# Softmax reciprocals repeated through DRAM, and the value product of a pair ahead of the next score products

## The reference

```python
h = rmsnorm(x, norm_scale)
q, k, v = h @ wq, h @ wk, h @ wv            # 16 heads of 64
weights = softmax((q * 64 ** -0.5) @ k.T)   # per head, 256 x 256, float32
new_vals = weights @ v
x = layernorm(x + new_vals @ w_out + b_out)
```

## Time and profile before

| | us |
|---|---|
| median of 3 runs | 1432.15 (1431.54 to 1432.47) |
| the profiled execution | 1431.51 |
| its span | 1429.7 |

### The profile page before, as it was taken

How to read it: one execution, slowest core, us unless ns; L and a number is a source line. 1 busy time by engine, 2 the same in 40 slices (tenths; PEclk the granted TensorE clock), 3 DMA queues, 4 the chain that set the end, 5 groups by cost and what they waited for, 6 DMA issues and landing times.

```text
span 1429.7 us, 33458 instructions
## 1 busy us (share of the span) xinstructions
PE 1366.9 (96%) x11456; PEld 1202.2 (84%) x11456; DVE 925.6 (65%) x2535; ACT 904.3 (63%) x2492; POOL 502.5 (35%) x409
## 2 busy tenths in 40 slices
PE   6897999999999999999999999999999999999867
PEld 4685989888898988889898898988889898888767
DVE  4366576675766757566675757667576675756684
ACT  6675766757577575766657576675757657575423
POOL 3307062350705316071440706235070531607100
PEclk9999999999999999999999999999999999999988
DMA  7000000000000000000000000000000000000000
GB/s 262 5 1 5 1 2 8 0 7 0 0 7 0 7 0 0 7 0 7 0 7 0 0 7 0 7 0 7 0 0 7 0 7 0 0 5 1 5 1 8
DMA packets 13944, 13.77 MB, mean 10 GB/s; under 512 B 1609, under 2 KB 12754, under 8 KB 13650
## 3 DMA queue, kind: packets, MB, share of 16 engines
q1 hardware_dynamic: 13906, 13.27, 2.9%
HBM read 11.17 MB, written 2.10 MB: 9 GB/s over the span
## 4 chain that ended last, share of the span: by engine, by line
PE 64%; issue 11%; DVE 8%; ACT 4%; DVEq 4%; POOL 3%; POOLq 2%; SPq 1%; DMA 1%; ACTq 0%
PE bank_F L1208 14%; PE bank_S L1081 6%; DVEq L346 4%; PE bank_T L1067 4%; PE bank_T L1122 4%; PE bank_A L1135 4%; PE bank_T L1068 3%; PE bank_T L1069 3%; PE bank_F L1067 3%; ACT probs L573 3%; PE bank_F L1068 3%; PE bank_F L1069 3%; PE bank_A L1146 3%; PE bank_A L1067 3%; PE bank_A L1068 3%
## 5 line engine op out<-in xcount | busy, mean ns | idle before, releaser
L1208 PE MATMUL bank_F<-down,hid 128*128 128x128 f32 x2944 | 357.5, 277 | 5.4 <-DVE x L790 4.6
L1208 PEld LDWEIGHTS bank_F<-down,hid 128*128 128x128 f32 x2944 | 342.0, 192 | 14.7 <-DVE x L790 8.3
L573 ACT ACTIVATE probs<-bank_S,neg_max 128x256 f32<-128x256 f32 x512 | 236.2, 476 | 140.7 <-DVE neg_max L711 140.7
L711 DVE TENSOR_REDUCE neg_max<-bank_S 128x2 f32<-128x512 f32 x256 | 164.6, 684 | 96.1 <-PE bank_S L1081 96.0
L790 DVE SCALAR_TENSOR_TENSOR x<-bank_F,gates,x 128x128 f32<-128x128 f32 x496 | 149.8, 343 | 42.5 <-PE bank_F L1208 32.6
L491 POOL TENSOR_TENSOR hid<-hid,qkv 128x1024 f32<-128x1024 f32 x60 | 169.2, 2831 | 22.6 <-ACT hid L589 22.6
L461 POOL TENSOR_TENSOR mean_sq<-sum_sq,one_over_d 128x2 f32<-128x2 f32 x16 | 3.1, 197 | 442.8 <-ACT h_row L547 442.8
L552 ACT ACTIVATE probsT<-bank_T 128x512 f32<-128x512 f32 x256 | 139.6, 606 | 27.8 <-PE bank_T L1122 27.8
L479 POOL TENSOR_TENSOR hid<-qkv 128x1024 f32<-128x1024 f32 x45 | 121.1, 2690 | 69.3 <-ACT qkv L552 69.3
L1146 PE MATMUL bank_A<-probsT,values 128*64 128x256 f32 x1024 | 139.6, 394 | 1.1 <-ACT probsT L552 1.0
L1122 PE MATMUL bank_T<-ident,probs 128*128 128x128 f32 x1024 | 138.3, 278 | 0.2 <-ACT probs L573 0.2
(11 more groups left out here) (187 smaller groups left out, 3133.2 us busy)
## 6 DMA issues: line engine op xcount, KB each, us to landing
x_row<-in_x SPq DMA_DIRECT2D x16, 128.0 KB, 2.2
hid<-in_w SPq DMA_DIRECT2D x1, 2048.0 KB, 9.1
down<-in_w SPq DMA_DIRECT2D x1, 2048.0 KB, 14.3
out<-x SPq DMA_DIRECT2D x16, 128.0 KB, 1.8
hid<-in_rw SPq DMA_DIRECT2D x1, 1024.0 KB, 7.3
hid<-in_wv SPq DMA_DIRECT2D x1, 512.0 KB, 3.9
hid<-in_wq SPq DMA_DIRECT2D x1, 512.0 KB, 5.1
hid<-in_wk SPq DMA_DIRECT2D x1, 512.0 KB, 5.8
```

The lines of the kernel that those rows point to most:

```text
L573: ins = sc.activation(probs[:, h // 2 % 2, h % 2, t, :], unit.bank(f"S{h}")[:, t * S:(t + 1) * S], ACT.Exp, bias=neg_max[:, h, t:t + 1], a ...
L711: ve.tensor_reduce(neg_max[:, h, :], v.bank(f"S{h}")[:, :].rearrange("p (t k) -> p t k", t=NT), AX.X, ALU.max, negate=True).then_inc(max_r ...
L1208: ins = te.matmul(bank[:, (j * NT + t) * P:(j * NT + t + 1) * P], hid[:, e, k, tokens(t)], down[:, e, k, :], start=k == 0, stop=k == m - 1)
```

## The change

Four edits:

1. In `pe_units`, `O{s-1}` stands ahead of `S{2s+2}` and `S{2s+3}` instead of behind them.
2. `spread` and `repeat_inverse` are gone. SP carries the reciprocals: it stores the 128 x 4 values of a pair to DRAM in the order head, query (`sums_apart`, 2 KB in elements of 4 bytes), waits until they are there, and loads each head's 256 values to 64 partitions with two transfers (`inv_spread`, 64 KB each).
3. `o_out` is gone. VectorE multiplies the value product straight from PSUM by `inv_spread`, and so waits for the value product and for the two transfers instead of for ScalarE.
4. SP's program is written out for all 18 iterations instead of looped, and the two largest loads of weights (2 MB each) start from ScalarE's queue in step 0 of iteration 0.

```diff
     for s in range(HP):
         put("A", "QK2", on=a and s == 0)
+        put("A", f"O{s - 1}", on=a and s >= 1)
         put("S0", f"S{2 * s + 2}", on=a and s + 1 < HP)
         put("S1", f"S{2 * s + 3}", on=a and s + 1 < HP)
-        put("A", f"O{s - 1}", on=a and s >= 1)
...
+            def spread_inverse(v, s):
+                sp.wait_ge(inverse_ready, v.at(0, HP, s + 1))
+                if v.it > 0 or s >= 2:
+                    sp.wait_ge(inverse_spread, v.at(0, 32 * HP, 32 * max(s - 1, 0)))
+                sp.dma_start(sums_apart[s % 2].rearrange("j (t p) -> p (j t)", t=NT), sum_inv[:, s % 2, :], allow_slow_non_contiguous=True).then_inc(inverse_stored, 16)
+                sp.wait_ge(inverse_stored, v.at(0, 16 * HP, 16 * (s + 1)))
+                if s >= 2:
+                    sp.wait_ge(*v.drain(f"O{s - 2}"))
+                elif v.it > 0:
+                    sp.wait_ge(*v.previous().drain(f"O{HP - 2 + s}"))
+                for j in range(2):
+                    src = sums_apart[s % 2, j]
+                    sp.dma_start(inv_spread[j * DH:(j + 1) * DH, s % 2, :], bass.AP(src.tensor, src.offset, [[0, DH], [1, S]])).then_inc(inverse_spread, 16)
...
+                if v.a:
+                    for s in range(HP):
+                        spread_inverse(v, s)
...
-                        o_out(v, s - 1)
-                        repeat_inverse(v, s)
                         transposed_probs(v, s)
...
-                    if v.a and s >= 1 and s != HP - 2:
-                        o_out(v, s - 1)
-                    if v.a and s != HP - 2:
-                        repeat_inverse(v, s)
...
+                    if v.it == 0 and s == 0:
+                        for dst, src in loads1:
+                            act.dma_start(dst, src).then_inc(loaded[4], 16)
...
+                if v.it > 0 or s >= 2:
+                    dve.wait_ge(inverse_stored, v.at(0, 16 * HP, 16 * max(s - 1, 0)))
                 settled(dve, ve.reciprocal(sum_inv[:, s % 2, :], row_sum[:, s % 2, :]).then_inc(inverse_ready, 1))
 
             def o_scale(v, s):
 
-                dve.wait_ge(o_copied, v.at(0, HP, s + 1))
-                ve.tensor_tensor(oT(s), oT(s), v.bank(f"O{s}")[:, S:2 * S], ALU.mult).then_inc(v.drain(f"O{s}")[0], 1)
+                dve.wait_ge(*v.fill(f"O{s}"))
+                dve.wait_ge(inverse_spread, v.at(0, 32 * HP, 32 * (s + 1)))
+                ve.tensor_tensor(oT(s), v.bank(f"O{s}")[:, 0:S], inv_spread[:, s % 2, :], ALU.mult).then_inc(v.drain(f"O{s}")[0], 1)
...
-            def spread(v, s):
-                bank = v.bank(f"O{s}")
-                pe.wait_ge(*v.drain(f"O{s}", before=1))
-                pe.wait_ge(repeated_ready, v.at(0, HP, s + 1))
-                for t in range(NT):
-                    te.transpose(bank[:, S + t * P:S + (t + 1) * P], row_inv[:, s % 2, t].rearrange("p j e -> p (j e)"), ident[:])
```

More of the change, by code:

```diff
@@ L243, in transformer_blocks @@
         sum_inv = sb("sum_inv", P, 2, 2 * NT)
-        row_inv = sb("row_inv", P, 2, NT, 2, DH)
+        sums_apart = nc.dram_tensor("sums_apart", [2, 2, S], F32).ap()
+        inv_spread = sb("inv_spread", P, 2, S)
         oT_early = sb("oT_early", P, HP // 2, S)
@@ L314, in transformer_blocks @@
         inverse_ready = sem("inverse_ready")
-        repeated_ready = sem("repeated_ready")
-        o_copied = sem("o_copied")
+        inverse_stored = sem("inverse_stored")
+        inverse_spread = sem("inverse_spread")
         max_ready = sem("max_ready")
@@ L362, in weights_and_values @@
                     qkv1[:, t, :, 2, :].rearrange("p g (a d) -> p a d g", a=1).broadcast_to(full))
-        n_loads = [0] * 5
+        loads1 = (up1_loaded, w1_in), (down1[:], w2_in)
+        n_loads = [0, 0, 0, 0, 16 * len(loads1)]
         def wait_weights(eng, v, group):
@@ L408, in load_late @@
                 load(4, router1[:], router1_in)
-                load(4, up1_loaded, w1_in)
-                load(4, down1[:], w2_in)
+            def spread_inverse(v, s):
[11 more added lines that the diff above has]
+                    sp.dma_start(inv_spread[j * DH:(j + 1) * DH, s % 2, :], bass.AP(src.tensor, src.offset, [[0, DH], [1, S]])).then_inc(inverse_spread, 16)
             def body(v):
@@ L421, in body @@
                     sp.dma_start(out[v.it - 2 + v.step, :, :].rearrange("(t p) d -> p t d", p=P), x4[:]).then_inc(stored, 16)
-            run(sp, body)
+            for it in range(ROWS + 2):
+                body(Iteration(it, 0, banks))
             sp.wait_ge(stored, 16 * (ROWS + 1))
@@ L556, in v_out @@
                 copy_out(v, f"V{n}", values[:, t, half * 512:half * 512 + 512], v.bank(f"V{n}")[:, :])
-            def o_out(v, s):
-                act.wait_ge(*v.fill(f"O{s}"))
-                sc.activation(oT(s), v.bank(f"O{s}")[:, 0:S], ACT.Copy).then_inc(o_copied, 1)
             def qk_out(v, s):
@@ L620, in tail @@
                     gelu1(v, u)
-            def repeat_inverse(v, s):
-                act.wait_ge(inverse_ready, v.at(0, HP, s + 1))
-                sc.activation(row_inv[:, s % 2], sum_inv[:, s % 2].rearrange("p (j t a) -> p t j a", j=2, a=1).broadcast_to([P, NT, 2, DH]),
-                              ACT.Copy).then_inc(repeated_ready, 1)
             def transposed_probs(v, s):
@@ L673, in body @@
                     head_exp(v, 1)
-                if v.a:
-                    o_out(v, HP - 1)
                 sc.activation(table_load[:], table_load[:], ACT.Gelu)
@@ L1138, in unit @@
                     s = int(name[1:])
-                    if s >= HP - 2:
-                        spread(v, s)
                     for j in range(2):
@@ L1225, in body @@
                 for name, bank in (pe_units(v.it) if v.it >= 0 else PRE):
-                    if name[0] == "S" and bank == "S0" and v.nth.get(f"O{int(name[1:]) // 2 - 2}"):
-                        spread(v, int(name[1:]) // 2 - 2)
                     free, count = v.drain(name, before=1)
```

## The result

The changed kernel took 2093.34 us (median of 4 runs, 2088.18 to 2095.43) against 1432.31 us for the kernel before (1431.54 to 1433.03): a ratio of 1.461 [1.4581, 1.4638]. The sign of the forecast was right; its size, 1462 us in a range of 1436 to 1484, was not.

What follows compares the result with a forecast made beforehand. TensorE, at work 84.46 of 84.90 us, was held in several steps by a chain through VectorE. +4.8 (iteration 0), +1.9 (iteration 1) and 14 x 1.7 = 23.8 made +30.5 on 1431.5: 1462 us, range 1436 to 1484.

Steps and rivals of the forecast that it cites:

- The order: Value product ahead of the next scores lengthens steps 1, 3, 4 and 5: +1.7 us an iteration; chance 0.68 with transfers hidden.
- Rule A: In each step `QK{s+3}` starts at least 2.96 us after the scores; in step 1 the down product at least 4.16.
- Rule B: Value product waits for copies of transposed weights, 4.72 us after the next pair's scores; score products at least 5.74 us apart.
- The first rows: Iterations 0 and 1, with few or no fill units: +4.8 us and +1.9 us.
- The weights' traffic: Weights' loads in iteration 0 add up to 2 us of traffic there; taken as none.
- the store: SP's store of a pair's 512 reciprocals to DRAM, issue to landing: 3.2 us, bounds 1.8 and 8.4.
- its queue keeps up: SP is busy about 3.8 us a pair and pairs come at least 4.9 us apart, so its queue does not fall behind.
- Its own sign of being wrong: Prediction wrong if the iteration is under 84.9 us, or VectorE waits for a transfer at `o_scale` in the loop.
- the way is too slow: Rival: way through DRAM over 8.5 us, each further us paid in each of 16 iterations, up to 1505 us; chance 0.14.
- pair 7: Pair with least time: 8.5 us from reciprocals to VectorE's scaling, against 6.0 for the way through DRAM, so no cost.
- The removed work: Rival: TensorE's removed transposes, 2.5 us an iteration, are the whole effect: 40 us less, 1392 us; chance 0.12.
- Balance: Rival: VectorE starts maxima earlier, the loop's waits come to 2.5 us and cancel the gain: 1431 us; chance 0.06.

Runs made afterwards that it cites:

- The kernel with a cheap store: Changed kernel with each pair's sums stored as 128 pieces of 16 bytes instead of 512 of 4 (reciprocals reach wrong columns): 1472.77 us, ratio 1.0299.

## Why the prediction was wrong

**The order: right, and in size.** The kernel with a cheap store is the one that the forecast describes, so its timeline of PE can be laid beside the table of steps. Its value products in one iteration, which answer to the earlier trace rows, and the waits inside its steps 1, 3 and 4:

```profile
357.41 1.08 PE L1142 MATMUL bank_A<-probsT,values 128*64 128x256 f32 x8 [0.21 <-ACT probsT L571]
358.43 0.39 PE L1087 MATMUL bank_S<-qk_hi,qk_lo 64*128 64x256 f32 x2
...
361.37 0.38 PE L1073 MATMUL bank_A<-hT_hi,wq_lo 128*128 128x256 f32 x1 [0.79 <-DVE qk_lo L736]
362.57 2.05 PE L1204 MATMUL bank_F<-down,hid 128*128 128x128 f32 x16 [0.23 <-DVE x L796]
364.56 1.08 PE L1142 MATMUL bank_A<-probsT,values 128*64 128x256 f32 x8
...
372.09 1.08 PE L1142 MATMUL bank_A<-probsT,values 128*64 128x256 f32 x8
...
376.05 0.39 PE L1073 MATMUL bank_A<-hT_hi,wq_lo 128*128 128x256 f32 x1 [0.73 <-DVE qk_lo L736]
...
378.25 1.08 PE L1142 MATMUL bank_A<-probsT,values 128*64 128x256 f32 x8
...
382.21 0.39 PE L1073 MATMUL bank_A<-hT_hi,wq_lo 128*128 128x256 f32 x1 [0.95 <-DVE qk_lo L736]
...
384.90 1.08 PE L1142 MATMUL bank_A<-probsT,values 128*64 128x256 f32 x8
...
390.61 1.08 PE L1142 MATMUL bank_A<-probsT,values 128*64 128x256 f32 x8 [0.91 <-ACT probsT L571]
...
395.56 1.08 PE L1142 MATMUL bank_A<-probsT,values 128*64 128x256 f32 x8
...
401.21 1.08 PE L1142 MATMUL bank_A<-probsT,values 128*64 128x256 f32 x8
```

| Step | 1 | 2 | 3 | 4 | 5 | 6 | 7 |
|---|---|---|---|---|---|---|---|
| forecast, us | 7.46 | 7.44 | 6.06 | 6.57 | 5.74 | 4.94 | 5.59 |
| with 16-byte pieces, us | 7.36 | 7.53 | 6.16 | 6.65 | 5.71 | 4.95 | 5.65 |

(Step 1 is measured as 364.56 - 357.41 and the 0.21 of waiting ahead of it.) Rule A: from the scores of step 1, at 358.43, to `QK4` it is 2.94 us, to the down product 4.14, forecast 2.96 and 4.16. Rule B: the value product that opens step 6 waits 0.91 us for the copies of its transposed weights, and the scores ahead of it and behind it are 5.71 us apart (385.91 and 391.62), forecast 5.74. The iteration is 86.7 us (86.8 without any store), forecast 86.6.

**The first rows: under-sized.** Scores of iteration 0 stand 6.3 us apart on average with 16-byte pieces (26.15 to 57.70, five steps), against the forecast 5.74: about 3 us more than the 4.8 of the sum. The weights' traffic, which the prediction had at nothing, is not needed to explain this: with no store at all the scores stand 6.3 us apart as well (25.86 to 57.56), and there TensorE's value products wait for ScalarE's copies, not behind a transfer. (With 16-byte pieces one of the five steps, 7.01 us long, does stand behind one.) What the two have in common is the clock. It is granted at 0.88 in these stretches, where before it was 1.00 (24.88 to 48.89); without a store the one step of the five with a granted clock of 1.00 takes 5.79 us, close to rule B's 5.74, and the other four, at 0.74 to 0.92, take 6.3 to 6.7. In all the cheap store's kernel came to 1472.8 us, 11 above the forecast, inside its range. In its profiled execution, 1469.3 us, it is 7 above; by the time at which the first row is stored (245.78 us, 13.9 later than before, where the sum has 8.4) some 5 of these lie in the first rows.

**The step that failed: the store, and with it "its queue keeps up".** The term was 3.2 us, bounds 1.8 and 8.4. In the trace it is 9.42 in the median, three times the value and above the upper bound. The bound was worked from 128 elements of 4 bytes in 2.1 us, times four for four times the elements. The runs show that the count is a small part: 512 elements far apart take 2.16. What the row lacked was any instance of many small writes side by side in DRAM; moreover it is a load, not a store. The upper end had no ground, since no row bore on it at all. (The 3.8 us a pair that the text gives for SP are 4.1 by its own terms, 3.2 and two issues of 0.43; this changes nothing.) Its own sign of being wrong was seen: VectorE waits for a transfer at `o_scale` all through the loop.

**A second fault lies in the price of that bound.** The rival "the way is too slow" was given 1505 us at the upper end, from the latency of pair 7 alone, though the text says that SP falls behind from 5 us on. Had the store's bound been put through SP's loop, the sum would have been there: 8.4 + 1.2 for the issues is 9.6 us a pair, 77 us for eight pairs. With the cheap store the eight pairs last 45 us, so 32 us an iteration are missing, some 510 in sixteen, and the time is 1462 + 510, about 1970 us. With 9.4 it is 10.6 us a pair, 84.8 for eight, 39.8 over the 45, and 39.8 x 16 = 637 us; the runs put 620 on the store. So the way's latency is the small cost and its throughput the large one. The chance of 0.14 was given to the right mechanism with the wrong price.

**The sign was right for another reason.** "Slower" had 0.83, of it 0.68 for the order and 0.14 for late transfers. With the cheap store the order's kernel is 40 us above the one before; the change is 661 above it, and in it the new order is no slower than the old one (2093 against 2131 us). So that the sign came out right says little for the forecast.

**The clock.** The forecast had no term for it. In the iteration shown, 10.2 us of the 125.3 are the same instructions at 0.89 of the clock. They don't seem to add to the length, since SP sets it: TensorE is idle for 32 us besides, and what the iteration has beside its pairs is no longer than at a clock of 1.00 (41.2 and 41.8 us). In iteration 0 the clock is the likely missing term.

**The count of pieces.** The Trainium skill, "DMA: Bandwidth & Descriptors", section "Rules for kernel authors", says that a non-contiguous last dimension becomes one descriptor per element. The packets agree: 49152 fewer with four elements to a piece. The prediction set against this rule a row that shows no cost per element, and followed the row. Yet the rule's count isn't the price either: with the same 512 pieces the kernel takes 1476 us if they lie 64 bytes apart, and 2093 side by side. The same page of the Trainium skill, section "Specifications", says that below 512 bytes the DMA engines read, modify and write; no run here shows such a step, and the pieces of 16 bytes, far below that size too, cost 1.41 us.

**The other rivals.** The removed work doesn't decide in the changed kernel but is worth 2% by itself with a cheap store in the old order (1405 us, by the rival 1392). Balance held nowhere.

## What to carry to other kernels

A transfer that one queue must wait out before it issues the next is a serial loop: price its latency plus its issues times the number of times per iteration against the iteration, besides asking whether one of them is in time. Where the trace has no transfer of the same form (piece size, distance of the pieces in DRAM), give its price no upper bound from another form, and store in pieces that are as long as the consumer's access pattern can undo: in the old order, 8 bytes instead of 4 turned a ratio of 1.489 into 0.9914. And an instruction moved ahead of another takes its cover away: measure what the work between two units covers before the order is changed.

## What the runs showed of the hardware

- A store of 2 KB to DRAM, from its issue to the issue of the load that waits for it: 1.41 us in 128 pieces of 16 bytes, 2.16 in 512 pieces of 4 bytes that lie 64 bytes apart, 9.42 in 512 side by side (medians).
- Half as many small writes side by side take as long as all (9.52 and 9.42 us).
- Two loads of 64 KB each that repeat a row of 1 KB over 64 partitions, read from DRAM: landed in 2.8 us in the median with a cheap store ahead, 3.6 in the changed kernel.
- TensorE's granted clock was 1.00 in loop iterations with waits of up to 0.95 us, and 0.89 in one with waits of 4.4 to 7.4 us; a value product behind such a wait took 1.97 us instead of 1.08, at a granted clock of 0.50. In iteration 0, with waits of 0.86 to 2.78 us and no fill units, it was 0.88.
- VectorE's transpose takes about as long for 128x32 as for 32x32: 212 and 202 ns.
- VectorE's and GpSimd's products over 128x1024 float32 in SBUF didn't run at the same time: VectorE's, 1.22 us with GpSimd idle, ended 1.08 us after GpSimd's when that one was under way, and so took up to 3.4 us, and GpSimd's took 3.35 us instead of 2.36 when VectorE's was there first.
